# Moving one projection step ahead of the head transposes, and loading half of the last layer's weights early

## What is computed

```python
# D = 1024, N_HEADS = 16, hd = 64, x: [8, 4096, 1024]
def _L0_attn_ref(x, Wq, Wk, Wv, Wo, bo):
    q = (x @ Wq.T).reshape(N, S, H, hd).transpose(0, 2, 1, 3)   # k, v likewise
    att = jnp.einsum('nqhd,nkhd->nhqk', q, k)
    att = jax.nn.softmax(att / jnp.sqrt(hd), axis=3)
    out = jnp.einsum('nhqk,nkhd->nqhd', att, v).reshape(N, S, D)
    return out @ Wo.T + bo

def _L0_ffn_ref(x, ...):
    def step(c, xt):
        ft = jax.nn.sigmoid(xt @ wf.T + c @ uf.T + bf)
        it = jax.nn.sigmoid(xt @ wi.T + c @ ui.T + bi)
        gt = jnp.tanh(xt @ wc.T + c @ uc.T + bc)
        return ft * c + it * gt, None
    c_final, _ = lax.scan(step, c0, x)
    return jnp.tanh(jnp.einsum('tbi,oi->tbo', x, wo) + c_final @ uo.T + bo)

x = x + _layernorm(_L0_attn_ref(_layernorm(x), ...))
x = x + _layernorm(_L0_ffn_ref(_layernorm(x), ...))
```

## Time and profile before

| | |
|---|---|
| median of 2 runs | 3597.24 us (3576.68 and 3617.81) |
| the profiled execution | 3559.77 us, its span on the slowest core (core 4) 3558.2 us |
| spans of the 8 cores | 3521.1 to 3558.2 us |
| busy: PE, DVE, ACT, POOL | 55%, 29%, 16%, 9% of the span |
| setup and first batch's projections | about 0 to 168 us |
| attention of 8 batches, with the last projections | about 168 to 2000 us |
| recurrent weights, then the layernorm loop | 2000 to 2233 us |
| scan | 2239 to 2961 us |
| output layer | 2991 to 3262 us |
| final layernorm | 3262 to 3558 us |

### The profile page before, as it was taken

How to read it: one execution, slowest core, us unless ns; L and a number is a source line. 1 busy time by engine, 2 the same in 40 slices (tenths; PEclk the granted TensorE clock), 3 DMA queues, 4 the chain that set the end, 5 groups by cost and what they waited for, 6 DMA issues and landing times.

```text
span 3558.2 us, 31866 instructions; the slowest of 8 cores (3521.1 to 3558.2 us)
## 1 busy us (share of the span) xinstructions
PE 1969.8 (55%) x9540; PEld 930.9 (26%) x9540; DVE 1014.3 (29%) x1754; ACT 554.0 (16%) x1257; POOL 332.7 (9%) x510
## 2 busy tenths in 40 slices
PE   1666445555454555454543112899999996886000
PEld 0323222222222222222221001344444442332000
DVE  0434333333333333333432013222211221222222
ACT  1011111111111111111111046211111111111000
POOL 1010101001101001011011201000000001000111
PEclk9766666666666666666656555899999998999555
DMA  7010211111112112111021676100000003111333
GB/s 116 24 47 23 57 42 47 34 42 48 51 37 56 33 38 54 42 47 51 29 53 51 108 170 175 31 1 12 12 12 13 12 12 60 33 30 45 120 119 115
DMA packets 167406, 186.99 MB, mean 53 GB/s; under 512 B 109886, under 2 KB 122174, under 8 KB 167230
## 3 DMA queue, kind: packets, MB, share of 16 engines
q0 software_dynamic: 53456, 151.38, 16.4%
q1 hardware_dynamic: 113792, 33.57, 3.9%
HBM read 151.68 MB, written 58.72 MB: 59 GB/s over the span
## 4 chain that ended last, share of the span: by engine, by line
PE 51%; DVE 15%; DMA 12%; issue 8%; ACT 7%; another core or an unknown queue 4%; DVEq 1%; POOL 1%; ACTq 0%; POOLq 0%; SPq 0%
PE ps_p L1581 11%; PE ps_a L2029 10%; PE ps_a L2035 9%; DMA xin<-x 7%; PE ps_p L1445 5%; PE ps_p L2122 3%; PE ps_p L2129 3%; DVE otn L1747 3%; PE ps_a L1698 2%; DVE kst L1650 2%; DVE qst L1650 2%; DMA vst<-v_scr 2%; PE ps_rl L1731 2%; ACT pt_sb L1710 2%
## 5 line engine op out<-in xcount | busy, mean ns | idle before, releaser
L1710 ACT ACTIVATE pt_sb<-ps_a 128x512 bf16<-128x512 f32 x128 | 76.0, 594 | 1010.0 <-PE ps_a L1698 1010.0
L1731 PE MATMUL ps_ot<-pt_sb,vst 128*65 128x128 bf16 x256 | 63.0, 279 | 288.7 <-DMA vst<-v_scr 242.4
L2049 ACT ACTIVATE gat<-ps_a,biases 128x512 f32<-128x512 f32 x192 | 131.9, 687 | 583.1 <-PE ps_a L2035 583.1
L2059 DVE TENSOR_TENSOR cT<-cT,gat 128x512 f32<-128x512 f32 x64 | 44.3, 692 | 578.7 <-ACT gat L2049 578.7
L1445 PE MATMUL ps_p<-wo_sb,zlT_t 128*128 128x512 bf16 x512 | 174.6, 516 | 49.4 <-DVE zlT_t L1431 49.4
L1581 PE MATMUL ps_p<-wq_sb,xlnT_t 128*128 128x512 bf16 x512 | 181.6, 532 | 33.5 <-DVE xlnT_t L1567 33.5
L2029 PE MATMUL ps_a<-xtT_sl,wq_sb 128*128 128x512 bf16 x512 | 133.5, 408 | 49.8 <-DMA xtT_sl<-xt_scr 44.2
L2122 PE MATMUL ps_p<-qst,gat 128*128 128x512 bf16 x512 | 122.9, 383 | 58.0 <-DMA gat<-xt_scr 33.8
L1682 POOL DMA_DIRECT2D vst<-v_scr x128 | 95.8, 753 | 529.2 <-DMA v_scr<-vtok 464.1
L2035 PE MATMUL ps_a<-zb,wk_sb 128*128 128x512 bf16 x512 | 125.8, 390 | 0.0
L1497 POOL DMA_DIRECT2D x<-x1t x32 | 17.9, 560 | 1138.4 <-DVE x1t L1487 895.1
(11 more groups left out here) (159 smaller groups left out, 2747.5 us busy)
## 6 DMA issues: line engine op xcount, KB each, us to landing
xin<-x POOLq DMA_DIRECT2D x96, 512.0 KB, 5.1
xin<-xr POOLq DMA_DIRECT2D x32, 512.0 KB, 4.2
x<-x1t POOLq DMA_DIRECT2D x32, 512.0 KB, 3.0
out<-x1t POOLq DMA_DIRECT2D x32, 512.0 KB, 3.3
v_scr<-vtok SPq DMA_DIRECT2D x32, 256.0 KB, 2.0
vst<-v_scr POOLq DMA_DIRECT2D x128, 64.0 KB, 3.0
od<-orow SPq DMA_DIRECT2D x128, 64.0 KB, 1.8
zin<-od POOLq DMA_DIRECT2D x128, 64.0 KB, 3.0
```

The costliest lines, as they stand in the source:

```text
L1710: ch_exp.inc(sc.activation(pt_sb[:, gbuf * 512:(gbuf + 1) * 512], ps_a[:, abank * 512:(abank + 1) * 512], AF.Exp, scale=0.125))
L1731: inst = t.matmul(psot[0:65, pk4 * 128:(pk4 + 1) * 128], vst[:, vslot * 260 + pk4 * 65: vslot * 260 + (pk4 + 1) * 65], pt_sb[:, gbuf * 512 ...
L2049: ch_gev.inc(sc.activation(gat[:, gi * 512:(gi + 1) * 512], ps_a[:, pg * 512:(pg + 1) * 512], func, bias=biases[:, bcol + mt:bcol + mt + 1]))
```

## The change

1. The fourth `emit_P2` of a batch is emitted right after group 15, ahead of the head transposes of tiles 0 and 1 instead of behind them. For `n = 1` to `6` this changes the order on PE and DVE; for `n = 0` there is none, and for `n = 7` it stays where it was. `emit_P1_qtr` puts nothing on GpSimd's, ScalarE's or SyncE's list, so their order is as before.
2. Half 0 of the two output-layer matrices is loaded during the layernorm loop, into tiles that are free by then (`zin`, `zlT_t`, `vtok`, `pt_sb`, `vst`): 16 DMAs of 128 rows by 512 columns, four each behind the loads of tiles 4, 8, 12 and 16. `f_wol` loads half 1 alone. The matmuls of half 0 wait for the new semaphore instead of `ch_cd`, and read the new places.

```diff
@@ -1807,22 +1807,18 @@
                 emit_P1_front(n + 1, 0)
             if grp == 11 and n + 1 < B:
                 emit_P1_front(n + 1, 1)
-            if grp % 4 == 3 and grp < 15 and n >= 1:
+            if grp % 4 == 3 and n >= 1:
                 emit_P2(n - 1, grp // 4, ODS_hist[n - 1])
         ODS_hist[n] = (ch_ods[0].n, ch_ods[1].n)
         g_vld_hist[n] = tuple(_c.n for _c in ch_vld)
         if n + 1 < B:
             emit_P1_qtr(n + 1, 0)
             emit_P1_qtr(n + 1, 1)
-            if n >= 1:
-                emit_P2(n - 1, 3, ODS_hist[n - 1])
             emit_P1_front(n + 1, 2)
             emit_P1_qtr(n + 1, 2)
             emit_P1_front(n + 1, 3)
             emit_P1_qtr(n + 1, 3)
             stk_vsp[n + 1] = (ch_stk.n, (ch_vsp[0].n, ch_vsp[1].n))
-        elif n >= 1:
-            emit_P2(n - 1, 3, ODS_hist[n - 1])
 
     for rt in range(4):
         emit_P2(B - 1, rt, ODS_hist[B - 1])
@@ -1872,6 +1868,12 @@
     ch_hev = c("hev")
     ch_hst = c("hst")
     ch_ho = c("ho")
+    ch_wol = c("wol", 16)
+    wo0_slices = ([zin[:, i * 512:(i + 1) * 512] for i in range(4)]
+                  + [zlT_t[:, i * 512:(i + 1) * 512] for i in range(4)])
+    uo0_slices = ([vtok[:, i * 512:(i + 1) * 512] for i in range(4)]
+                  + [pt_sb[:, i * 512:(i + 1) * 512] for i in range(2)]
+                  + [vst[:, 0:512], vst[:, 512:1024]])
 
     def g_fconsts(g, apj=A_PJ, aam=A_AM, az=A_Z):
         g.wait_ge(ch_pj.sem, apj)
@@ -1975,6 +1977,21 @@
         P("sync", f_sp)
         ch_trd[buf].bump()
         ftrd_hist.append((ch_trd[buf], ch_trd[buf].n))
+
+        if tt in (4, 8, 12, 16):
+            ci = (tt - 4) // 4
+            def f_wol0(g, ci=ci):
+                for k in range(4):
+                    j = ci * 4 + k
+                    if j < 8:
+                        dst, wsrc, jj = wo0_slices[j], wd["woT2"], j
+                    else:
+                        dst, wsrc, jj = uo0_slices[j - 8], wd["uoT"], j - 8
+                    ch_wol.inc(g.dma_start(
+                        out=dst, in_=wsrc[jj * 128:(jj + 1) * 128, 0:512]))
+            P("gpsimd", f_wol0)
+            ch_wol.bump(4)
+    WOL0 = ch_wol.n
     LN3 = tuple((ch.sem, ch.n) for ch in ch_trd)
 
     def f_cinit(v, fc_=FCONSTS):
@@ -2072,7 +2089,7 @@
     ch_cbf.bump()
     CFIN = ch_cbf.n
 
-    for fc in range(2):
+    for fc in (1,):
         def f_wol(g, fc=fc, sg=SCAN_G):
             g.wait_ge(ch_g.sem, sg)
             ch_cd.inc(g.dma_start(
@@ -2111,10 +2128,13 @@
             ph = (rt * 2 + fc) % 2
 
             def f_hmm(t, rt=rt, buf=buf, fc=fc, ph=ph, bsl=bsl, xrl=XRL,
-                      cfin=CFIN, wol=WOL, hev=(ch_hev.n - 1)):
+                      cfin=CFIN, wol=WOL, wol0=WOL0, hev=(ch_hev.n - 1)):
                 t.wait_ge(xrl[0].sem, xrl[1])
                 t.wait_ge(ch_cbf.sem, cfin)
-                t.wait_ge(ch_cd.sem, wol)
+                if fc == 0:
+                    t.wait_ge(ch_wol.sem, wol0)
+                else:
+                    t.wait_ge(ch_cd.sem, wol)
                 if hev > 0:
                     t.wait_ge(ch_hev.sem, hev)
                 psh = ps_h[ph]
@@ -2122,6 +2142,7 @@
                     t.matmul(psh[:, :],
                              xr_sl[:, buf * 1024 + ft * 128:
                                    buf * 1024 + (ft + 1) * 128],
+                             wo0_slices[ft] if fc == 0 else
                              wo_sl[:, fc * 4096 + ft * 512:
                                    fc * 4096 + (ft + 1) * 512],
                              start=(ft == 0), stop=False)
@@ -2129,6 +2150,7 @@
                     t.matmul(psh[:, :],
                              cT_bf[:, m2 * 512 + bsl * 128:
                                    m2 * 512 + (bsl + 1) * 128],
+                             uo0_slices[m2] if fc == 0 else
                              uo_sl[:, fc * 4096 + m2 * 512:
                                    fc * 4096 + (m2 + 1) * 512],
                              start=False, stop=False)
```

## The result

The changed kernel takes 3502.45 us (median of 11 runs), the kernel before 3576.72 us (10 runs, the two shown ahead of the prediction among them). The ratio is 0.9809, with a 95% interval of 0.9782 to 0.9837: 68 us less by the ratio, with 58 to 78 us in the interval. Some executions of either kernel are disturbed and some per cent longer; ratios and traces here are of undisturbed ones. The profiled execution's span is 3502.2 us on its slowest core, core 5.

What follows compares the result with a forecast made beforehand. No engine was taken as the bound throughout; what counts is where PE and DVE both stand still. Terms: -59.5 - 10.5 + 4 = -66 us, factor 0.9815, taking the median 3597.2 to 3530 us; range 3490 to 3570 us.

Steps and rivals of the forecast that it cites:

- The boundary: Six batch boundaries: with the projection step ahead of the head transposes, eight copies fill DVE's wait; 59.5 us less.
- The wait less 0.28 us: Gain per batch boundary: DVE's wait before the normalisation shrinks to 0.28 us; 61.2 - 6 x 0.28 = 59.5 us.
- The gap: Between scan and output layer: loading half 1 alone lets PE start earlier; 10.5 us less, ends 10 and 12.
- The loop: Layernorm loop: 16 early weight loads add 1 us per group of four, 4 us in all, ends 0 and 20.
- the group moves mostly between the two: Layernorm loop: four early loads, 3 us of transfer, move mostly between tile 4's and tile 5's loads; 1 us cost.
- issuing is hidden: Layernorm loop: issuing four early loads takes GpSimd 2.1 us, within its 3.23 us of idleness between two tiles' loads.
- The clock: The q matmuls behind the boundary wait: no gain or loss from PE's clock counted, +6 or -6 us in the range.
- No gain and no loss: At the boundaries, transposes filling the wait were counted as leaving the q matmuls' time unchanged, give or take 6 us.
- The clock did not gain: Rival at the boundaries: q matmuls run at 2.4 GHz, up to 11 us more gain, -77 us in all; chance 0.10.
- The boundary did not gain half: Rival at the boundaries: head copies don't run as one block, so -30 us there, -36 us in all; chance 0.08.
- The small loads overlap: Rival in the layernorm loop: the 16 loads don't overlap, 3.8 us each, +61 us, total -9 us; chance 0.05.
- The projection step did not find `zin` missing: Rival at the boundaries: the moved projection step waits 12.83 us for `zin` each time, +11 us in all; chance 0.03.

Runs made afterwards that it cites:

- half-moved run: The kernel before, with the fourth projection step put between the head transposes of tile 0 and those of tile 1; ratio 0.9916 to the kernel before.

## Why the prediction was right, and where it was not

Forecast was -66 us, a factor of 0.9815; measured is 0.9809, -68 us. The mechanism was right, but that the two numbers agree so closely is in part luck. The three terms came out as -59.4, -12.0 and +8.0 us, in sum -63.4 instead of -66; two stages that the forecast left alone took 3.8 us more, so -60 us is what the stages show. The profiled execution of the kernel before was also a quick one: the mean of its cores' spans is 3536.3 us, where the executions behind the ratios have 3547 to 3559 us on average, while the changed kernel's profiled execution (3485.0 us) is like its others (3481.5 us). That can explain why the ratio shows more than the stages; in which stage the difference lies is not known. The forecast median of 3530 us was 28 us too high, mostly since it stood on the median of two runs, which is 20 us above the median of ten. By the prediction's own steps:

- **The boundary.** "The wait less 0.28 us", 59.5 us: measured 59.4 us, and 57.3 us with this part alone. DVE's wait before the normalisation fell by 58.3 us over the six boundaries (mean of the cores), so the mechanism carries the gain; the last microseconds of the agreement are luck, as the same code gives 1999.3 and 2004.1 us for this stage. The size could be forecast because the boundary after batch 0 had already shown the new order, copies and all, in the old trace. The half-moved run supports that the gain follows the copies in the wait; in its profiled execution some 11 us went back into other waits.
- **The gap.** Forecast -10.5 us, ends 10 and 12; measured -12.0 us. The right term was the pace of the queue: two 1 MB pieces less at 6 us each. The difference of two landings in the earlier trace rows, 10.2 us, was too small because the first two pieces had shared the engines with the third. On the slowest cores the pieces of half 0 landed 16.1 us after the second was issued, and alone those of half 1 take 15.0 us; the second is issued 0.7 us sooner as well. With 10.2 us this makes the 12.0. That sharing the engines is the reason for the 1.1 us is argued, not shown.
- **The loop.** Forecast +4 us, ends 0 and 20; measured +8.0 us. The step that failed is "the group moves mostly between the two" loads: I took 1 us of the 3 us of transfer as uncovered, and the rows show 2.8 us at tile 5, 2 us a group over the loop. The loop had slack on the DMA engines on average (59% busy) but none at the place where the group was put, right ahead of the next load. That issuing is hidden was right.
- **The clock.** "No gain and no loss" was right: 5.60 us for the q matmuls before, 5.47 us after. The reason beside it was wrong. I took the 0.50 during the head transposes as a sign that transposes do not bring up the clock, as the Trainium skill has it in TensorE: Matmul & The Clock Gate, Part 4. The run with extra transposes contradicts this with a granted clock of 1.00. In the old order as in the new one PE paused 0.39 us before most sets, and once these pauses were filled, with either kind of operation, the clock rose. A row can agree with a rule for another reason. One small gain was overlooked: the projection steps' own matmuls (line 1445) keep PE busy 168.5 us instead of 171.0, and DVE waits 2.4 us less for them.
- **The rivals.** The clock did not gain. The boundary did not gain half. The small loads overlap: 16 of them, with 1/32 of the bytes, cost 0.9 us, within the scatter. So the fixed part of 2 us each, which the Trainium skill gives in DMA: Bandwidth & Descriptors, in the anatomy of one DMA, does not add up in this queue. The projection step did not find `zin` missing: DVE's copy behind its transposes starts 0.20 us after the scaling before it, as in the rows above.

## What to carry to other kernels

Where an engine stands still at a place that returns in every pass, look for work of its own list that doesn't depend on what it waits for, and move the start of the chain ahead of it; the gain here was the smaller of the wait and that work, and a pass in which the chain is missing shows it beforehand. Prefetches belong where the DMA engines have long free stretches (here the scan), not into a loop that waits for its own loads, even if these engines are 40% free on average. And look at what stands in front of a load in its queue's list: a store that waits for a result cost more here (some 130 us in each of two stages) than the order of the computation (some 59 us).

## What the runs showed of the hardware

- TensorE's clock rose from 1.2 to 2.4 GHz on transposes alone, once they ran without the pauses of 0.39 us between sets (granted clock 1.00 instead of 0.50), and was at the low level again after a pause of 3.30 us.
- 16 DMAs of 128 x 16 columns, put into the queue of a loop bound by its loads, cost that loop 0.9 us in all, no more than its scatter; with 128 x 512 columns each they cost 8 us, half a microsecond a DMA.
- 16 to 32 DMAs with conversion to bfloat16, landing in other tiles of the memory from which a scan reads its operands, did not slow it, though PE is busy 94% of that time: 721.4 us before, 720.9 to 721.6 us with them.
